# A graph network on one core: the hidden product in six one-pass parts, transposes and the second weight product moved one step earlier

## The reference

```python
H  = (adj != 0)                       # 1024 x 1024, zeros and ones
Dn = 1 / (H @ adj[0]); Be = 1 / H.sum(0)
def conv(v, W, b):                    # hypergraph convolution
    return Dn * (H @ (Be * (H.T @ (v @ W.T)))) + b
h  = layer_norm(relu(conv(x, W1, b1)), gamma, beta)     # 512 wide
x1 = norm(x + conv(h, W2, b2) + x)
agg = (adj @ x1) / max(adj.sum(-1), 1e-6)
out = norm(x1 + relu(concat(x1, agg) @ WL.T))
```

## Time and profile before

| | |
|---|---|
| median of 3 runs | 1109.9 us (1109.59 to 1110.53) |
| profiled execution | 1110.66 us, its span 1108.6 us |
| TensorE busy | 1093.2 us, 99% |
| VectorE busy | 699.6 us, 63% |
| ScalarE busy | 314.9 us, 28% |
| GpSimd busy | 182.5 us, 16% |

### The profile page before, as it was taken

One profiled execution on the slowest core, in us unless ns is written; L12 is line 12 of the kernel. 1 busy time (PEld: TensorE's weight loads), 2 busy tenths in 40 slices (PEclk: granted clock), 3 DMA queues, 4 the chain that ended last, 5 costly groups with the idle time before them and its releaser, 6 DMA issues.

```text
span 1108.6 us, 18544 instructions
## 1 busy us (share of the span) xinstructions
PE 1093.2 (99%) x6112; PEld 899.0 (81%) x6112; DVE 699.6 (63%) x1846; ACT 314.9 (28%) x705; POOL 182.5 (16%) x256
## 2 busy tenths in 40 slices
PE   7999999999999999999999999999999999999997
PEld 6879697796978969688796887969789697887966
DVE  4665595665955768548685486754766646856326
ACT  4342302422124221333113331143301433024220
POOL 0222004120031202211031110401104020041000
PEclk9999999999999999999999999999999999999999
DMA  7017612067211572124611445115442075300001
GB/s 280 20 39 153 150 41 58 0 151 152 55 40 31 120 151 57 38 65 101 146 47 38 96 102 121 41 38 129 103 89 71 4 151 115 65 9 1 1 1 39
DMA packets 64599, 86.18 MB, mean 78 GB/s; under 512 B 9024, under 2 KB 54720, under 8 KB 64576
## 3 DMA queue, kind: packets, MB, share of 16 engines
q1 hardware_dynamic: 63520, 85.88, 33.6%
q10 hardware_dynamic: 1056, 0.00, 0.1%
HBM read 77.47 MB, written 8.39 MB: 77 GB/s over the span
## 4 chain that ended last, share of the span: by engine, by line
PE 94%; DVE 4%; DMA 1%; ACT 0%; issue 0%; ACTq 0%; DVEq 0%
PE bank L731 40%; PE bank L802 10%; PE bank L840 10%; PE bank L862 10%; PE bank L824 10%; PE bank L759 10%; PE bank L832 3%; PE bank L848 1%; DVE adjT L539 1%; DMA small<-in_L_gnn_gamma_dram 1%; DVE HT L544 1%; PE bank L768 1%; DVE o_f L676 0%; DVE xres L680 0%; ACT m_hi L389 0%
## 5 line engine op out<-in xcount | busy, mean ns | idle before, releaser
L731 PE MATMUL bank<-yv,adjT 128*128 128x257 f32 x1024 | 223.3, 380 | 0.0
L731 PEld LDWEIGHTS bank<-yv,adjT 128*128 128x128 f32 x1024 | 194.1, 190 | 31.3 <-issue 3.8
L394 ACT ACTIVATE small<-mv,small 128x1 f32<-128x1 f32 x192 | 56.6, 295 | 362.6 <-DVE mv L521 266.9
L759 PE MATMUL bank<-x_hi,H 128*128 128x258 f32 x512 | 122.8, 289 | 0.8 <-DVE m_lo L526 0.8
L731 PE MATMUL bank<-x_hi,H 128*128 128x256 f32 x512 | 122.6, 283 | 0.0
L731 PE MATMUL bank<-m_hi,HT 128*128 128x256 f32 x512 | 121.6, 281 | 0.0
L731 PE MATMUL bank<-x_lo,H 128*128 128x256 f32 x512 | 121.1, 281 | 0.0
L731 PE MATMUL bank<-m_lo,HT 128*128 128x256 f32 x512 | 120.9, 280 | 0.0
L526 DVE SCALAR_TENSOR_TENSOR m_lo<-bank,small,m_hi 128x256 fp32r<-128x256 f32 x128 | 61.1, 483 | 94.2 <-ACT m_hi L389 94.1
L824 PE MATMUL bank<-W1T,zT 128*128 128x512 f32 x256 | 120.4, 593 | 0.0
L840 PE MATMUL bank<-gW2T,xnT 128*128 128x256 f32 x512 | 119.8, 380 | 0.0
(11 more groups left out here) (80 smaller groups left out, 1621.7 us busy)
## 6 DMA issues: line engine op xcount, KB each, us to landing
raw<-in_adj_dram SPq DMA_DIRECT2D x112, 256.0 KB, 8.5
adjB<-in_adj_dram SPq DMA_DIRECT2D x224, 128.0 KB, 3.4
x_in<-in_x_dram SPq DMA_DIRECT2D x28, 256.0 KB, 4.5
out_dram<-xres SPq DMA_DIRECT2D x112, 64.0 KB, 1.6
raw<-in_adj_dram SPq DMA_DIRECT2D x4, 1024.0 KB, 12.9
w_row<-in_adj_dram SPq DMA_DIRECT2D x8, 512.0 KB, 3.7
x_in<-in_x_dram SPq DMA_DIRECT2D x1, 1024.0 KB, 7.1
out_dram<-xres SPq DMA_DIRECT2D x4, 256.0 KB, 2.2
```

Source lines behind the costliest of these rows:

```text
L394: nc.scalar.activation(std[:, i:i + 1], mv[:, which, i, 1:2], ACT.Sqrt, bias=eps_c)\
L731: last = mm(bank(stage, i)[:, 0:n_cols], lhsT, rhs, start=(k == 0 and part == 0), stop=(k == NT - 1 and part == parts - 1))
L759: last = mm(*args, start=(c == 0 and n == 0), stop=(c == NT - 1 and n == 1))
```

## The change

P is computed from three products of parts of about 12 bits. W1 is split once at the start: `W1_high` (W1 scaled by 1 - 1/8192 and rounded to float32r), `W1_low` (the rest, times 4096) and `W1_cross` = W1_high - W1_low scaled. z is split for each graph in the same way: ScalarE writes `z_high`, VectorE `z_low`, then `z_cross` = z_high - 4096 z_low. P(s) is now z_high W1_high + z_low W1_low (four one-pass products); a new stage M(s) holds z_cross W1_cross (two). hidden = rDn (1 + 1/4096) P - (rDn / 4096) M + b1: ScalarE takes M out of PSUM with its scale into `hbias`, GpSimd adds b1 in place, and VectorE adds this to P times its scale, in the place where b1 stood.

The step order is new: M(s), P(s), Q(s - 3), TH(s - 2), with five of the eight rounds of S2's second chunk ahead of step 0 and three ahead of step 1. On ScalarE and VectorE the work of a step is reordered. The last Q stands behind S3's second round, and S3 accumulates four tiles together. `hrow` has three slots for four. The banks are given out anew. In memory, `xnT` lies where w_row is, so the load of w_row stands behind the first quarter of `raw`, behind Q's last tile. `hbias` lies in the second half of `x_lo`, so GpSimd's split of Q(4) waits until P's last tile is out of PSUM.

```diff
-    "P": (0, 1, 2, 0, 1, 2, 0, 1),
-    "Q": (3, 4, 5, 3, 4, 5, 3, 4),
+    "P": (0, 1, 0, 1, 0, 1, 0, 1),
+    "M": (2, 3, 2, 3, 2, 3, 2, 3),
+    "Q": (4, 5, 4, 5, 4, 5, 4, 5),
...
-SECOND_CHUNK = {0: (0, 1, 2), 1: (3, 4), 2: (5, 6), 3: (7,)}
-LAG_T = 3
-LAG_Q = 4
-H_SLOTS = 4
+SECOND_CHUNK = {0: (0, 1, 2, 3, 4), 1: (5, 6, 7)}
+LAG_T = 2
+LAG_Q = 3
+H_SLOTS = 3
...
 # SyncE, each graph
-                    sp.wait_ge(dn_ready, b * NT + NT)
-                    load_w(b + 1)
                     sp.wait_ge(xb_ready, b * NT + NT)
                     sp.wait_ge(x_split, b * NT + NT)
                     load_x(b + 1)
                     sp.wait_ge(*full("Q", NT - 1, b))
-                    load_graph(b + 1)
+                    load_raw(b + 1, 0)
+                    load_w(b + 1)
+                    for j in range(1, NT // 2):
+                        load_raw(b + 1, j)
...
 # GpSimd, setup, then each graph
+            for d in range(ND):
+                pool.wait_ge(W1_high_done, d + 1)
+                nc.gpsimd.tensor_tensor(W1_low[:, d, :], W1T[:, d, :], W1_high[:, d, :].bitcast(F32), ALU.subtract)\
+                  .then_inc(W1_low_done, 1)
...
+                for s in range(NT + LAG_Q):
+                    if s < NT:
+                        pool.wait_ge(*emptied("M", s, b))
+                        nc.gpsimd.tensor_tensor(hbias[:, s % 2, :], hbias[:, s % 2, :], b1_row[:, :], ALU.add)\
+                          .then_inc(hbias_done, 1)
+                    if s > LAG_Q:
+                        split_q(s - LAG_Q - 1)
+                split_q(NT - 1)
...
 # ScalarE, each graph (take_z_high: two activations of 128x512 with scale=ROUND_DOWN)
+                take_z_high(0)
+                act.wait_ge(rDn_ready, b * 2 + 2)
                 for s in range(NT + LAG_Q):
+                    if s == max(SECOND_CHUNK):
+                        take_z_high(1)
                     if s < NT:
+                        act.wait_ge(*full("M", s, b))
+                        empties_bank(nc.scalar.activation(hbias[:, s % 2, :], bank("M", s)[:, :], ACT.Identity,
+                                                          scale=rDn_cross[:, s:s + 1]), "M", s)
+                    if s > LAG_Q:
+                        take_x_hi(s - LAG_Q - 1)
                     if 0 <= s - LAG_T < NT:
                         i = s - LAG_T
                         act.wait_ge(*full("TH", i, b))
                         empties_bank(nc.scalar.activation(xnT[:, i % 2, :, :].rearrange("p k c -> p (k c)"),
                                                           bank("TH", i)[:, :], ACT.Copy), "TH", i)
+                    if 0 <= s - 1 < NT:
+                        root("h", 0, std_h, s - 1, b)
                     if s < NT:
+                        act.wait_ge(*emptied("P", s, b))
+                        nc.scalar.activation(hrow[:, s % H_SLOTS, :], hrow[:, s % H_SLOTS, :], ACT.Relu)\
+                          .then_inc(relu_done, 1)
+                take_x_hi(NT - 1)
...
 # VectorE, each graph
+                take_z_low(0)
+                take_z_cross(0)
                 for s in range(NT + LAG_Q):
+                    if s == max(SECOND_CHUNK):
+                        take_z_low(1)
+                    if s > LAG_Q:
+                        take_q(s - LAG_Q - 1)
+                    if 0 <= s - 1 < NT:
+                        dve.wait_ge(relu_done, b * NT + s)
+                        moments("h", 0, hrow[:, (s - 1) % H_SLOTS, :], s - 1, b)
                     if s < NT:
                         dve.wait_ge(*full("P", s, b))
+                        dve.wait_ge(hbias_done, b * NT + s + 1)
                         empties_bank(nc.vector.scalar_tensor_tensor(
+                            out=hrow[:, s % H_SLOTS, :], in0=bank("P", s)[:, :], scalar=rDn_main[:, s:s + 1],
+                            in1=hbias[:, s % 2, :], op0=ALU.mult, op1=ALU.add), "P", s)
                     if 0 <= s - 1 < NT:
                         inverse_root("h", std_h, rstd_h, s - 1, b)
                         centre("h", 0, hrow[:, (s - 1) % H_SLOTS, :], rstd_h, s - 1, b)
+                    if s == max(SECOND_CHUNK):
+                        take_z_cross(1)
+                take_q(NT - 1)
...
 # TensorE, each graph
+                for s in range(NT + LAG_T):
                     for k in SECOND_CHUNK.get(s, ()):
                         s2_step(1, k)
                     if s < NT:
+                        pe.wait_ge(*free("M", s, b))
...
+                        for d in range(ND):
+                            last = mm(bank("M", s)[:, :], z_cross[:, d, nodes], W1_cross[:, d, :],
+                                      start=(d == 0), stop=(d == ND - 1))
+                        fills_bank(last, "M", s)
                         pe.wait_ge(*free("P", s, b))
                         for d in range(ND):
-                            last = mm(bank("P", s)[:, :], zT[:, d, s * P:(s + 1) * P], W1T[:, d, :],
-                                      start=(d == 0), stop=(d == ND - 1))
+                            mm(bank("P", s)[:, :], z_high[:, d, nodes], W1_high[:, d, :], start=(d == 0), stop=False)
+                            last = mm(bank("P", s)[:, :], z_low[:, d, nodes], W1_low[:, d, :],
+                                      start=False, stop=(d == ND - 1))
                         fills_bank(last, "P", s)
+                    i = s - LAG_Q
+                    if 0 <= i < NT - 1:
+                        take_product_Q(i)
                     i = s - LAG_T
...
                 tiled("S3", b, D, lambda c: pe.wait_ge(q_split, b * NT + c + 1), 2,
-                      lambda c, e, part: (H_columns(c, e), (x_hi, x_lo)[part][:, c, 0:D]))
+                      lambda c, e, part: (H_columns(c, e), (x_hi, x_lo)[part][:, c, 0:D]),
+                      group=4, behind_k=lambda c: take_product_Q(NT - 1) if c == 1 else None)
```

More of the change, by code:

```diff
@@ L606, in graph, with take_z_low @@
                 dve.wait_ge(bias_loaded, 16 * 2)
-                dve.wait_ge(rDn_ready, b + 1)
-                for s in range(NT + LAG_Q):
+                dve.wait_ge(rDn_ready, b * 2 + 2)
+                def take_z_low(ch):
+                    for d in range(ND):
+                        dve.wait_ge(z_high_done, b * (NCH * ND) + ch * ND + d + 1)
+                        cols = slice(ch * CH, (ch + 1) * CH)
+                        empties_bank(nc.vector.tensor_tensor(
+                            z_low[:, d, cols], bank("S2", ch * ND + d)[:, :], z_high[:, d, cols].bitcast(F32),
+                            ALU.subtract), "S2", ch * ND + d)
@@ new lines, in take_z_cross, with take_q @@
+                def take_z_cross(ch):
+                    for d in range(ND):
+                        dve.wait_ge(*emptied("S2", ch * ND + d, b))
+                        cols = slice(ch * CH, (ch + 1) * CH)
+                        nc.vector.scalar_tensor_tensor(
+                            out=z_cross[:, d, cols], in0=z_low[:, d, cols].bitcast(F32), scalar=-SPLIT,
+                            in1=z_high[:, d, cols].bitcast(F32), op0=ALU.mult, op1=ALU.add).then_inc(z_cross_done, 1)
+                def take_q(i):
+                    dve.wait_ge(*full("Q", i, b))
+                    if i >= 2:
+                        dve.wait_ge(q_split, b * NT + i - 1)
+                    empties_bank(nc.vector.tensor_tensor(q_f32[:, i % 2, :], bank("Q", i)[:, 0:D],
+                                                         bW2_row[:, :], ALU.add), "Q", i)
@@ L737, in tiled @@
                     ready(k)
-                    for i in range(GROUP):
+                    for i in range(group):
                         if k == 0:
@@ L741, in tiled @@
                         one(i, k)
[L742 removed]
+                    if behind_k:
+                        behind_k(k)
+                for i in range(group, NT):
                     if i == NT - 1 and before_last:
@@ L814, in graph, with take_product_Q @@
                 pe.wait_ge(HT_ready, b * NT + NT)
-                for s in range(NT + LAG_Q):
+                def take_product_Q(i):
+                    pe.wait_ge(*free("Q", i, b))
+                    pe.wait_ge(*emptied("TH", i, b))
+                    for k in range(NH):
+                        last = mm(bank("Q", i)[:, 0:D], xnT[:, i % 2, k, :], gW2T[:, k, :],
+                                  start=(k == 0), stop=(k == NH - 1))
+                    fills_bank(last, "Q", i)
+                for s in range(NT + LAG_T):
                     for k in SECOND_CHUNK.get(s, ()):
@@ L834, in graph @@
                         fills_bank(last, "TH", i)
-                    i = s - LAG_Q
-                    if 0 <= i < NT:
-                        pe.wait_ge(*free("Q", i, b))
-                        pe.wait_ge(*emptied("TH", i, b))
-                        for k in range(NH):
-                            last = mm(bank("Q", i)[:, 0:D], xnT[:, i % 2, k, :], gW2T[:, k, :],
```

(2 more changed lines are left out.)

152 lines of the change are left out of this document (83 added, 69 removed), and 8 rows, old and new, of the table PRODUCT_BANKS.

## The result

The changed kernel takes 1127.28 us (median of 4 runs, 1126.18 to 1128.50), the kernel before 1110.09 beside it: a ratio of 1.0156, 95% interval 1.0144 to 1.0168. It is slower by 17.2 us, for a forecast of 1125.

The account below looks back on a forecast made before the run. TensorE, busy 99% of the span, was taken to bound the kernel. Added costs of 10 us over 8 graphs, 3.5 for the load and 1 for setup, 14.5 in all, gave 1125 us, range 1106 to 1148.

Parts of the forecast that it names:

- The saving: M and P of a tile as six one-pass products: 1.40 us for 1.72, saving 2.56 us a graph.
- TensorE's busy time: Sign over the whole kernel: TensorE busy about 1073 us or less after the change.
- The start: Before TH(0), TensorE stands still until VectorE's late centring of tile 0 ends: 1.95 us a graph.
- my walk: Step through the engines' queues from the end of S2's first half, adding durations and hand-overs to find TensorE's waits.
- The end: Q(5) and Q(6) each wait 0.93 us for ScalarE's copy behind their transposes: 1.87 us a graph.
- Together: Start and end waits less the saving: 1.26 us more a graph, 10 us in 8.
- G: Length of GpSimd's new addition over 512 columns, taken as 1.35 us; the loop costs from 1.42 on.
- The load and S4: Next graph's later loads delay sums and m_lo, so S4 waits: 0.5 us in 7 graphs, 3.5 in all.
- Setup: Extra ScalarE passes over W1 and GpSimd additions while TensorE is transposing: 1 us, ends 0 and 3.
- The saving arrives: Rival: TH(0) is in time and the drain hides the copies; under 2.5 us standing a graph, 1090 us; chance 0.17.
- GpSimd sets the pace: Rival: GpSimd's addition takes 1.6 to 1.8 us, TensorE stands before every TH; 1139 to 1153 us; chance 0.20.
- Nothing in sum: Rival: the start's wait is half of that forecast and S4 never waits; 1109 us; chance 0.06.

Follow-up runs that it names:

- e7: Changed kernel with M one step ahead of P, lags 3 and 4, second chunk spread over steps 0 to 2, Q(7) in the loop: 1103.52 us.
- e5: Kernel before, with its fp32 P, but lags of 2 and 3 and Q(7) among S3's first products: 1130.91 us.
- e2: Changed kernel with GpSimd's addition of b1 left out: 1122.26 us.
- e3: Changed kernel with GpSimd's addition of b1 done twice in a row: 1211.44 us.
- e6: Changed kernel with DN_LAG 5 instead of 3, so VectorE takes the next graph's sums two tiles later: 1125.99 us.
- e8: Changed kernel with GpSimd's eight setup additions of b2 done on 8 columns instead of 256: 1127.23 us.
- e1: Changed kernel with lags of 3 and 4 steps again, four hrow slots, and TH ahead of Q in a step: 1137.38 us.
- e4: Changed kernel with M one step ahead of P, and hbias and its addition moved ahead with it: 1130.74 us.
- e10: e7 with M back in its own step in front of P, lags and spread chunk kept: 1134.85 us.
- e11: e7 with GpSimd's addition of b1 left out: 1101.81 us.

## Why the prediction was right, point by point

- **The saving.** Six products a tile at 0.2335 us, as reckoned: in the changed kernel P's products follow each other by 0.23 (198.69, 198.92), and a step of the loop takes 3.55 us (3.57). The Trainium skill's 216 ns for an isolated product (TensorE: Matmul & The Clock Gate, "Back-to-back issue gap") isn't what the trace shows here; the measured 233 decides.
- **TensorE's busy time: a sign that failed.** It was to be 1073 us or less and is 1082.0. The three holes are 1.47 + 0.78 + 0.69 = 2.94 us as idle time and 3.66 from product to product (next points); the 0.72 between counts as busy, 5.8 us in eight graphs of the 9 that are too many. e7, with the same products and fewer holes, has 1074.3. The rest I did not assign.
- **The start.** 1.95 us was predicted. From product to product it is 200.78 - 198.92 - 0.23 = 1.63, and the step behind it is 0.24 longer than the others, since TH(1) comes late in its turn (3.79 from M to M for 3.55): 1.87. VectorE's scaling of P(1) began 0.3 us earlier than in my walk, which had added up hand-overs that overlap in part: z_high starts at 196.27, before relu ends at 196.36. And TensorE restarted 0.05 us behind the centring (200.73 to 200.78), where I had 0.15.
- **The end.** 1.87 predicted; (1.38 - 0.44) + (1.29 - 0.44) = 1.79. e5 has the same two holes in a kernel without the split.
- **Together** 1.26 a graph was predicted, 1.26 measured. That it agrees so exactly is partly luck: start and end give 3.66 for my 3.82, and 0.16 a graph elsewhere, which no run assigns, makes up for it.
- **GpSimd.** G was 1.35 by estimate and is 1.338 in the mean: 1.29 alone, 1.68 to 1.69 when it begins while z_cross runs. My own sum gave 1.32 before I rounded it up. The Trainium skill (GPSIMD Engine Reference, "3.1 Elementwise — side-by-side cycle accounting") gives 4497 ns for an fp32 addition over 2048 columns and no fixed part for GpSimd; a quarter of it is an estimated 1.12, 0.17 under the undisturbed row. The overlap made no hole in the changed kernel, e2 and e3 show how near it is: no addition -5 us, two +84, part of it the clock's.
- **The load and S4.** 3.5 predicted, 2.5 measured (15.59 to 15.97 for 15.45, 7 graphs), by the mechanism named: the product at 246.02 waits 0.17 for an m_lo whose place on VectorE is behind sums that waited for raw or w_row. e6 takes it away by their place alone.
- **Setup: mis-sized.** I took 1 us, ends 0 and 3; it is 3.5 (1.3 + 1.9 + 0.2). The new GpSimd work was priced only where TensorE transposes. The term missed is what it does to VectorE: W_cross at 29.21 stretched a sum from 1.22 to 2.31 and an H tile from 0.69 to 1.75, and the additions of b2's row, which no longer wait for rDn, ran from 43.50 beside four sums. The second part is shown by e8; the first (1.3 us in S1) is read from the traces only: 2.31 and 1.75 stand in all eleven kernels with this setup, while the 1.3 scatters.
- **The last graph: missed**, 0.8 us. Its hole before TH(0) is 2.15 for 1.47, in e6 and e8 2.16. VectorE's first scaling starts 0.5 us behind the end of GpSimd's addition; only this graph's code is outside the loop. It is 0.51 or 0.52 us in the last graph of each of the nine kernels with the addition (the changed one, e1, e3, e4 and e6 to e10), and 0.03 or 0.04 in every other graph. Without the addition the last graph is hardly longer than the others (P to Q 32.76 for 32.63 in e2, 32.84 for 32.78 in e11), so it is the wait for GpSimd that is lengthened. What lengthens it stays open.
- **Rivals.** "The saving arrives" decides at 2.5 us of standing time a graph; there were 3.66. "GpSimd sets the pace" needed 1.6 us or more in every step; it happens in one of eight. "Nothing in sum" needed half of the start's wait and none in S4; the start's was 1.87 of 1.95, and S4 did wait.

Net of both errors, 2.5 us more in the setup, 0.8 in the last graph, 1.0 less in S4, the profiled 1127.5 is 14.5 + 2.3 over before's.

## What to carry to other kernels

Where a step of the fastest engine gets cheaper, walk every queue again before its lags are touched: the engines behind it did not get cheaper, and here one more link in the chain needed a step more of distance, not less (e7, -6.5 us), while the shorter lags, with Q(7) in S3, cost 21 by themselves (e5). Taking one cause away moves the wait to the next reader of the same late result (e1, e4), so a single edit says little: try them together and then each taken back. And work given to GpSimd is to be priced at what VectorE has running beside it, too.

## What the runs showed of the hardware

**GpSimd and VectorE hold each other up, instruction by instruction.** The z_cross of a chunk is two VectorE instructions of 0.68 us, 1.28 together, with both inputs in SBUF. Beside a GpSimd addition already running the pair took 2.37 us (e4, the first of the two 1.77); where the addition began during the second of them, z_cross kept its 1.28 and the addition took 1.68 or 1.69 for 1.30 (changed kernel, all eight graphs). In the last graph of e7 the addition (994.40, 1.67 us) began during the first of the two. That one kept its 0.68, and the second took 1.75:

```profile
994.26 2.35 DVE L687 SCALAR_TENSOR_TENSOR z_cross<-z_low,z_high 128x512 fp32r<-128x512 f32 x2
```

The Trainium skill (SBUF — State Buffer, "Who interferes with whom") says that a VectorE instruction with two inputs in SBUF contends with a GpSimd instruction that reads SBUF, that the ports they share are an exclusive lock, and that the order of issue decides which of them blocks. By that rule e4's z_cross begins its work when the addition ends, at 201.87, and ends at 201.87 + 1.28 = 203.15; the trace agrees to 0.12 (203.03). The changed kernel's addition would run from 201.93, the end of z_cross, to 203.23; the trace agrees to 0.16 (203.07). One thing is left open: e4's addition, though it was first, took 1.50 for 1.30.

**A hole of the same length is followed by a lower TensorE clock in one execution and not in another.** First windows of e8, then of the changed kernel, both behind a hole of 2.15 to 2.16 us in the last graph (the two kernels differ in the setup alone), then of e3, in the second graph, behind 4.14 us (columns: us, PE, PEld, DVE, ACT, POOL busy, granted clock, DMA share, GB/s):

```profile
1018.00:1020.00 2.00, 2.00 (x7) 1.62 (x6) 1.53 (x4) 0.89 (x2) 1.49 (x1) 0.50 0.00 0
1020.00:1022.00 2.00, 2.00 (x8) 1.68 (x8) 1.84 (x5) 1.21 (x2) 0.33 (x1) 0.78 0.00 0
```

```profile
1018.00:1020.00 2.00, 1.42 (x9) 1.27 (x10) 2.00 (x4) 1.62 (x3) 0.90 (x1) 1.00 0.00 0
1020.00:1022.00 2.00, 2.00 (x11) 1.69 (x9) 1.48 (x5) 0.60 (x2) 0.79 (x1) 1.00 0.00 0
```

```profile
213.60:215.60 2.00, 1.94 (x7) 1.75 (x8) 1.93 (x5) 1.19 (x3) 1.33 (x1) 0.50 0.00 0
215.60:217.60 2.00, 2.00 (x7) 1.52 (x6) 0.33 (x2) 0.29 (x1) 1.62 (x2) 0.50 0.00 0
217.60:219.60 2.00, 2.00 (x7) 1.64 (x6) 1.85 (x5) 1.21 (x2) 0.20 (x1) 0.60 0.00 0
```

0.50 is the 1.2 GHz level. In e8 it cost the last graph 1.3 us (35.38 for 34.09). In e10 0.50 came even behind holes of 1.80 us before M(4), from 754 and from 890.5 us on, some 4 us each, while holes of 1.77 to 1.80 in four of its other graphs left the clock at 1.00. There the lower clock cost nothing: P to Q took 36.80 or 36.81 us in all six. The holes of 1.47 us in the changed kernel's loop never did this; e7's 2.69 us before its first M left the clock at 1.00 in its profiled run, e11's 2.67 at the same place brought 0.50 and 2.9 us more. In e7 the runs at a mean clock of 0.999 took 1102.2 and 1102.3 us, those at 0.997 1104.7 and 1105.1. So the holes of 1.8 to 2.7 us carried a price, nothing in e10's two graphs, 1.3 us in e8 and 2.9 in e11, that was paid only at times, and a gain of that size, as in e6 and e8, can be lost in it. In the prediction I charged nothing for the clock.
